# Cross-attention scores from full tiles: split keys and queries packed into 96 rows by way of HBM

## What is computed

```python
q = heads(rms_norm(hidden) @ cq_w, 16, 16)        # 16 heads of 16 dims, 112 queries
k, v = split(encoder_outputs @ ckv_w)             # 375 keys and values a batch
scores = einsum('bhqd,bhkd->bhqk', q / sqrt(16), k)
p = softmax(scores, axis=-1)
cross = einsum('bhqk,bhkd->bhqd', p, v) @ cdense_w
```

## Time and profile before

| | |
|---|---|
| median of 3 runs | 2347.46 us (2345.52 to 2348.16) |
| the profiled execution's own time | 2341.35 us |
| its span, first to last instruction | 2339.5 us |
| mean granted PE clock over the span | 0.982 |
| stage E, first group of scores of batch 0 to that of batch 31 | 539.7 us |

### The profile page before, as it was taken

The page is one execution under the profiler, slowest core; times in us unless marked ns, Lnnn a source line. Parts: engine busy times, 40 slices in busy tenths (PEclk is TensorE's granted clock), DMA queues, the critical chain, the costliest instruction groups (busy, mean ns, idle before and its releaser), DMA issues.

```text
span 2339.5 us, 46940 instructions
## 1 busy us (share of the span) xinstructions
PE 2202.4 (94%) x19542; PEld 1835.6 (78%) x19542; DVE 1338.8 (57%) x1919; ACT 1071.1 (46%) x1842; POOL 881.5 (38%) x738
## 2 busy tenths in 40 slices
PE   7999999999799999988999999997999999999998
PEld 6899987778666668877777777775888888888887
DVE  6656537787589975546666666663534444434332
ACT  5343434333177755534555555553543344334332
POOL 2210127767434324521222111110745455555553
PEclk9999999999899999988999999998999999999999
DMA  6343415556454446641111111102534344344331
GB/s 227 129 161 112 173 52 209 201 199 222 157 175 139 138 131 247 235 159 35 42 40 50 42 40 50 42 22 106 179 124 160 113 133 136 128 133 122 104 113 45
DMA packets 107602, 293.88 MB, mean 126 GB/s; under 512 B 14560, under 2 KB 19008, under 8 KB 100736
## 3 DMA queue, kind: packets, MB, share of 16 engines
q1 hardware_dynamic: 88672, 230.60, 29.9%
q0 software_dynamic: 18720, 60.29, 7.0%
HBM read 221.65 MB, written 69.18 MB: 124 GB/s over the span
## 4 chain that ended last, share of the span: by engine, by line
PE 79%; DVE 8%; ACT 7%; DMA 2%; issue 2%; POOL 1%; SPq 0%; POOLq 0%; DVEq 0%; ACTq 0%
PE ps L109 19%; PE ps L111 18%; PE ps L110 18%; PE ps L1625 4%; PE ps L1662 4%; PE ps L1644 3%; DVE f_arena L995 3%; ACT f_arena L1547 2%; PE ps L1164 2%; PE ps L627 2%; ACT f_arena L1112 1%; DVE f_arena L991 1%; PE ps L1175 1%; DVE f_arena L987 1%; ACT f_arena L1118 1%
## 5 line engine op out<-in xcount | busy, mean ns | idle before, releaser
L109 PE MATMUL ps<-r_arena 128*128 128x512 f32 (+6 forms) x2410 | 902.7, 375 | 28.4 <-DVE r_arena L177 14.2
L177 POOL TENSOR_TENSOR r_arena<-f_arena,r_arena 128x512 fp32r<-128x512 f32 (+1 forms) x438 | 589.1, 1369 | 857.9 <-ACT r_arena L1268 433.6
L111 PE MATMUL ps<-r_arena 128*128 128x512 f32 (+6 forms) x2410 | 882.6, 366 | 0.0
L110 PE MATMUL ps<-r_arena 128*128 128x512 f32 (+6 forms) x2410 | 882.1, 366 | 0.0
L109 PEld LDWEIGHTS ps<-r_arena 128*128 128x128 f32 (+2 forms) x2410 | 454.1, 188 | 120.8 <-issue 26.3
L111 PEld LDWEIGHTS ps<-r_arena 128*128 128x128 f32 (+2 forms) x2410 | 454.5, 189 | 66.2
L110 PEld LDWEIGHTS ps<-r_arena 128*128 128x128 f32 (+2 forms) x2410 | 455.0, 189 | 60.0
L199 ACT CAST r_arena<-f_arena 128x512 fp32r<-128x512 f32 x400 | 235.6, 620 | 172.6 <-PE ps L111 135.4
L1761 DVE TENSOR_REDUCE e_negmax<-ps 112x3 f32<-112x1125 f32 (+1 forms) x160 | 225.2, 1408 | 104.2 <-PE ps L1625 101.5
L1547 ACT ACTIVATE f_arena<-ps 125x1792 f32<-125x1792 f32 x96 | 159.8, 1665 | 98.3 <-PE ps L1647 97.8
L2047 DVE SCALAR_TENSOR_TENSOR f_arena<-f_arena,ps 128x512 f32<-128x512 f32 (+1 forms) x88 | 57.4, 652 | 235.2 <-ACT f_arena L1937 235.2
(11 more groups left out here) (201 smaller groups left out, 2738.3 us busy)
## 6 DMA issues: line engine op xcount, KB each, us to landing
f_arena<-weights SPq DMA_DIRECT2D x400, 256.0 KB, 3.0
f_arena<-rows SPq DMA_DIRECT2D x14, 1160.0 KB, 5.3
f_arena<-qk_rows SPq DMA_DIRECT2D x32, 448.0 KB, 3.9
f_arena<-mem_n SPq DMA_DIRECT2D x8, 1536.0 KB, 7.6
f_arena<-mem_e SPq DMA_DIRECT2D x32, 376.0 KB, 3.2
f_arena<-mem_t SPq DMA_DIRECT2D x16, 750.0 KB, 5.5
h_rows<-f_arena SPq DMA_DIRECT2D x7, 1160.0 KB, 4.8
f_arena<-h_rows SPq DMA_DIRECT2D x7, 1160.0 KB, 5.2
```

Source lines behind the costliest of these rows:

```text
L109: first = pe.matmul(out, w_hi, x_hi, start=start, stop=False)
L110: pe.matmul(out, w_hi, x_lo, start=False, stop=False)
L111: return first, pe.matmul(out, w_lo, x_hi, start=False, stop=stop)
L177: return engine.tensor_tensor(out, source, high.bitcast(F32), ALU.subtract)
```

## The change

Keys and queries of a batch are split once, into one pair of tiles (`e_kq_parts`, both scaled by 16 to the power of -1/4) without masks. SP writes the parts to two arrays in HBM (`k_rows`, `q_rows`) and reads them back in another arrangement: `e_keys` has, for each of the 8 head pairs, rows high, low, high of the even head (48 rows) and of the odd head (48 rows), `e_queries` rows high, high, low, with zeros for the other head's 48 rows. One matmul over 96 rows then adds all three products of a head. The columns of the key and query weights are permuted on the host so that a tile holds one parity of heads. The negative maxima go by a DMA into rows 96 and 97 of `e_queries` (the same rows of `e_keys` are ones), and a by-key matmul over 98 rows gives a pair of heads with its maxima.

```diff
-S_UNITS, KEY_UNITS = 5, 3
+S_UNITS, KEY_UNITS = 6, 6
+PAIRS, ROWS = HEADS // 2, 3 * CHD
+E_SCALE = float(CHD) ** -0.25
...
+        e_kq_parts = both(8192, (CT, CEVEN + SEQ))
+        e_keys = [rv(10144 + 3008 * i, (PAIRS, CEVEN)) for i in range(3)]
+        e_queries = [rv(at, (CT, PAIRS, SEQ)) for at in (4096, 5888, 19168)]
+        e_c_parts = both(20960, (CT, SEQ))
+        e_max_tok = [rv(25536 + 128 * i, (P,), SEQ) for i in range(2)]
+        e_max_t = rv(25792, (SEQ,))
+        key_units = [(t, c) for t in range(CT) for c in range(NKC)]
+        s_heads = [range(3 * u, 3 * u + 3) if u < 4 else range(2 * u + 4, 2 * u + 6) for u in range(S_UNITS)]
+        MAX_ROW = CT * ROWS
+        MAX_PLACES = 16
+
```

Four DMAs store a batch, eight place it, one places its maxima. Three buffers of each tile rotate:

```diff
+            def store(b, x, wide, into):
+                sp.dma_start(into[b, :, x].rearrange("t d (g s) -> (d g) t s", g=PAIRS), e_kq_parts[x][:, :, wide].bitcast(F32)).then_inc(
+                    e_stored.sem, 16)
+
+            def store_both(b):
+                for x, made in enumerate((e_kq_hi, e_kq_lo)):
+                    sp.wait_ge(made, e_split(b))
+                    store(b, x, keys, k_rows)
+                    store(b, x, queries, q_rows)
+
+            def place_keys(b):
+                sp.wait_ge(*stored(b))
+                into, done = e_keys[b % 3].rearrange("p g s -> p (g s)").bitcast(F32), e_placed[b % 2].sem
+                for t in range(CT):
+                    at = ROWS * t
+                    sp.dma_start(into[at:at + 2 * CHD], k_rows[b, t].rearrange("x d s -> (x d) s")).then_inc(done, 16)
+                    sp.dma_start(into[at + 2 * CHD:at + ROWS], k_rows[b, t, 0]).then_inc(done, 16)
+
+            def place_both(b):
+                if b < 3:
+                    sp.wait_ge(*e_cleared.at(1 if b == 1 else 3))
+                else:
+                    sp.wait_ge(e_st, KEY_UNITS * (b - 2))
+                place_keys(b)
+                into, done = e_queries[b % 3].rearrange("p t g s -> p t (g s)").bitcast(F32), e_placed[b % 2].sem
+                for t in range(CT):
+                    at = ROWS * t
+                    sp.dma_start(into[at:at + CHD, t], q_rows[b, t, 0]).then_inc(done, 16)
+                    sp.dma_start(into[at + CHD:at + ROWS, t], q_rows[b, t].rearrange("x d s -> (x d) s")).then_inc(done, 16)
+
+            def place_maximum(b):
+                sp.wait_ge(e_mxt_made, b + 1)
+                sp.dma_start(e_queries[b % 3][MAX_ROW:MAX_ROW + 2].bitcast(F32), e_max_t[0:2 * HEADS].bitcast(F32)).then_inc(
+                    e_max_placed.sem, 16)
+
...
             sp.wait_ge(*d_scattered.at(16 * BLOCKS))
             load_queries(0)
             load_queries(1)
+            place_keys(0)
+            sp.wait_ge(e_ones, 4 + 2 + 1)
+            sp.wait_ge(e_kq_hi, 2)
+            for row in (0, CHD):
+                place_queries(sp, row, e_kq_parts[0])
+            load_queries(2)
             base = sp.value_load(base_f[0:1, 0:1], min_val=W_F, max_val=W_F + F_CHUNKS)
-            for c in range(RING):
-                ring_load(sp, M_F + c, chunk_at(base, c))
-            for b in range(2, BATCHES):
-                load_memory(b)
-                load_queries(b)
+            store_both(1)
+            for s in range(BATCHES + 1):
+                if s + 4 < BATCHES:
+                    load_memory(s + 4)
+                if s + 3 < BATCHES:
+                    load_queries(s + 3)
```

```diff
                                         None).then_inc(e_scattered[b % 2].sem, 16)
 
+            e_memory_low(pool, 2)
+            pool.memset(e_queries[1].bitcast(F32), 0.0).then_inc(e_cleared.sem, 1)
+            pool.wait_ge(*e_cleared.at(1))
...
             for s in range(BATCHES + 2):
...
-                for x in range(2):
-                    dve.scalar_tensor_tensor(lo[:, :, x, :], ps[:, at:at + CT, CEVEN:CEVEN + SEQ], cmask[:, x:x + 1],
-                                             hi[:, :, x, :].bitcast(F32), ALU.mult, ALU.subtract).then_inc(e_kq_lo, 1)
+                dve.wait_ge(e_kq_hi, e_split(b) if wide.stop > CEVEN else 1)
+                dve.scalar_tensor_tensor(e_kq_parts[1][:, :, wide], ps[:, at:at + CT, wide], E_SCALE,
+                                         e_kq_parts[0][:, :, wide].bitcast(F32), ALU.mult, ALU.subtract).then_inc(e_kq_lo, 1)
```

The two kinds of scores, in 6 groups of heads (3, 3, 3, 3, 2, 2) and 6 by-key units of 4 matmuls. A unit uses two PSUM banks, in turn, so it waits for the unit two before it:

```diff
                 if u == 0:
-                    pe.wait_ge(e_kq_lo, 3 * (b + 1))
+                    pe.wait_ge(*placed(b))
                     if b == 0:
+                        pe.wait_ge(e_kq_lo, 2)
                         pe.wait_ge(e_v_act, 1)
                         pe.wait_ge(e_v_dve, 1)
                 if S_UNITS * b + u:
                     pe.wait_ge(e_maxed, S_UNITS * b + u)
-                if u == S_UNITS - 1 and b >= 2:
...
+                for h in s_heads[u]:
+                    last = pe.matmul(ps[0:SEQ, h - s_heads[u][0], 0:CEVEN], e_queries[b % 3][0:MAX_ROW, h % 2, h // 2, :],
+                                     e_keys[b % 3][0:MAX_ROW, h // 2, :], start=True, stop=True)
                 last.then_inc(e_s, 1)
...
             def scores_by_key(b, u):
...
+                    if b < 3:
+                        pe.wait_ge(*e_cleared.at((2, 4, 5)[b]))
+                    pe.wait_ge(*e_max_placed.at(MAX_PLACES * (b + 1)))
+                    pe.wait_ge(e_kq_lo, e_split(min(b + 3, BATCHES - 1)))
+                if u == 1:
+                    pe.wait_ge(e_v_act, min(b + 4, BATCHES))
+                    pe.wait_ge(e_v_dve, min(b + 4, BATCHES))
+                if b or u >= 2:
+                    pe.wait_ge(e_exp, KEY_UNITS * b + max(u - 1, 0))
+                t, c = key_units[u]
+                m = slice(c * KC, (c + 1) * KC)
+                for n in range(PAIRS // 2):
+                    pair = PAIRS // 2 * t + n
+                    last = pe.matmul(ps[0:KC, 4 + 2 * (u % 2) + n // 2, n % 2 * 2 * SEQ:(n % 2 + 1) * 2 * SEQ],
+                                     e_keys[b % 3][0:MAX_ROW + 2, pair, m], e_queries[b % 3][0:MAX_ROW + 2, :, pair, :],
+                                     start=True, stop=True)
                 last.then_inc(e_st, 1)
```

The maxima are written once into a tile of 128 columns instead of four times, and `maximum_turned` is a copy of 112 columns. ACT takes the exponentials of a batch in six instructions of 896 columns, the output's copy standing between the fourth and the fifth. PE's loop, which now splits keys two batches ahead and does both halves of a context together:

```diff
+            for s in range(BATCHES + 2):
+                old, now, new, by_key = s >= 2, s < BATCHES, s + 2 < BATCHES, 1 <= s <= BATCHES
+                if now:
+                    scores(s, 0)
+                if old:
+                    context(s - 2, 0)
+                    context(s - 2, 1)
...
+                if by_key:
                     maximum_turn(s - 1)
-                scores(s, 1)
-                if s >= 2:
-                    context(s - 2, 1)
-                if 2 <= s + 1 < BATCHES:
-                    values(s + 1, range(1))
-                if s >= 2:
+                if now:
+                    scores(s, 1)
+                if old:
...
+                if new:
+                    e_key_products(pe, s + 2)
+                if old:
                     back(s - 2)
-                scores(s, 2)
-                if s:
+                if now:
+                    scores(s, 2)
+                if new:
+                    queries_turn(s + 2)
+                    values(s + 2, range(NKC))
+                if now:
+                    scores(s, 3)
+                if by_key:
                     scores_by_key(s - 1, 0)
-                if s >= 2:
+                    scores_by_key(s - 1, 1)
+                if old:
                     dense(s - 2, 0)
-                scores(s, 3)
-                if s >= 2:
+                if by_key:
+                    scores_by_key(s - 1, 2)
+                if now:
```

```diff
+                if now:
+                    scores(s, 4)
+                if by_key:
+                    scores_by_key(s - 1, 3)
+                if old:
                     dense(s - 2, 1)
...
+                if now:
+                    scores(s, 5)
+                if by_key:
+                    scores_by_key(s - 1, 4)
+                    scores_by_key(s - 1, 5)
```

More of the change, by code:

```diff
@@ L1485, in build_xattn, with e_split, placed, stored @@
         e_out = [fv(18016 + 512 * i, (DIM,), SEQ) for i in range(2)]
-        e_k_parts = [both(8192 + 1504 * i, (CT, CEVEN)) for i in range(3)]
-        e_q_parts = [both(12704 + 896 * i, (QUADS, SEQ)) for i in range(3)]
-        e_c_parts = both(15392, (CT, SEQ))
-        e_max_tok = [rv(16288 + 128 * i, (4, 2 * HEADS), SEQ) for i in range(2)]
-        e_max_t = rv(16544, (QUADS, SEQ))
-        key_units = [[(0, 0), (0, 1)], [(0, 2), (1, 2)], [(1, 0), (1, 1)]]
-        s_heads = [range(3 * u, 3 * u + 3 if u < S_UNITS - 1 else HEADS) for u in range(S_UNITS)]
+        e_kq_parts = both(8192, (CT, CEVEN + SEQ))
[8 more added lines that the diff above has]
+        MAX_PLACES = 16
+        def e_split(b):
+            return b + 2
+        def placed(b):
+            return e_placed[b % 2].at(16 * (8 * (b // 2 + 1) + (2 if b % 2 == 0 else 0)))
+        def stored(b):
+            return e_stored.at(16 * (2 + 4 * b))
+        keys, queries = slice(0, CEVEN), slice(CEVEN, CEVEN + SEQ)
```

(26 more changed lines are left out.)

251 lines of the change are left out of this document (110 added, 141 removed).

## The result

The changed kernel takes 2288.98 us in the median of 4 runs (2287.28 to 2293.10), the kernel before 2347.81 in the median of 4 runs taken with it; the ratio is 0.9753, with a 95% interval of 0.9736 to 0.977. The forecast was 2283, faster; the range holds the result. So the two traces differ by 48.2 us of span, the medians by 58.8.

The account below looks back on a forecast made before the run. PE was taken to set the pace. 29 batches at 15.5 instead of 17.5 us give -58, start and end -6.4, together -64; from the median of 2347.46 the forecast is 2283 us, range 2258 to 2325.

Parts of the forecast that it names:

- The pass, 15.5 us: Steady batch on PE: 17.50 us falls to 15.5, with bounds 15.0 and 16.1.
- The short waits: New PE waits at reduces, between passes and before contexts: 0.25 us a batch in all.
- The rest of the pass: Keys, values, contexts, transposes and dense on PE: same instructions in another order, 10.01 us a batch.
- The rounds: Score matmuls on PE: 0.24 us per round of three 32-row tiles against 0.17 per full matmul, a gain of 0.6.
- The DMA: Added stores and placements in stage E: share 0.72, placement landing at 12 of 15.5 us, hidden with 3 to spare.
- Rival 2: Placement before a batch's scores is late, bound by partition: up to 20.3 us a batch, 2422 us; 18 in 100.
- Start and first passes: Stage E's beginning: first scores 2.7 us later, first two passes 26.5 us in place of 32.2, so -5.7.
- one more DMA (2.08 again): Start of stage E: batch 0's queries go through one further DMA of 2.08 us before the first scores.
- chains of reduces: First two passes, without contexts: reduces of 11.4 us and some 2 of other DVE work, 26.5 for both.
- The end, -3.4,: From the last batch's first scores to the last dense matmul: 35.5 us in place of 38.9.
- Rival 1: PE waits at several of the six reduces and at the contexts: 16.5 us a batch, 2312 us; 17 in 100.
- rival 3: By-key units still wait for each exponential in full: no change, within 5 us of 2347; 3 in 100.

Follow-up runs that it names:

- the first experiment: Changed kernel with by-key units again in pairs over all four banks, each next pair waiting for both exponentials; full tiles stay: 2349.69 us, 1.0008 of the kernel before.
- the second store: Changed kernel with each batch's split keys stored a second time, to another HBM array that nobody reads: 2325.01 us.
- another start: Changed kernel with batch 0's queries all placed from ACT's DMA queue and batch 1 split into tiles of its own: 2288.72 us.
- the new order and fillers: Changed kernel with score group five before by-key unit 2, six before dense's second half, and unused matmuls in passes 0, 1, 30 and 31: 2275.56 us, ratio 0.9718.

## Why the prediction was right

**The pass, 15.5 us.** Measured 15.36 in the steady passes, 15.53 in the mean of passes 2 to 30. A head's full matmul costs 0.17 as foreseen; a by-key matmul 0.109, between the bounds of 0.105 and 0.12. Two terms were off, and they nearly cancel. The short waits are 1.0 us a pass (0.3 at the exponential, 0.3 and 0.4 at reduces), where the forecast took 0.25. The rest of the pass is 9.0 us (15.36 - 2.72 - 2.62 - 1.04), where it took 10.01, since both halves of a context stand together (2.44 us from 1290.39 to 1292.83, where the halves took some 2.7) and the weight port idles at two changes of tiling a pass and not at six. That the sum came within 0.2 us is in part luck. That the gain hangs on the wait, the first experiment shows.

**The rounds, a reading that was wrong.** The prediction divided 0.71 us by three rounds, got 0.24 against 0.17 for a full matmul, and concluded that the tiles themselves gain 0.6 us by the rows. The 0.71 contains the 0.25 of idle weight port that the prediction itself names. Without it a round starts 0.17 us after the last. So 15 rounds before (three for each of the five groups) and 16 matmuls now stream 2.55 and 2.72 us: the full tiles lose 0.2 there, and gain at the changes of tiling.

**The DMA, the step that failed in size.** The forecast took 293 GB/s for the full share and got 0.72; measured are 0.89 to 0.90 at 218 GB/s. From the totals, 174 GB/s were added for 0.74 of the share, so the new transfers run at 235 GB/s. That rate leaves out any effect of the old and the new transfers on each other. The placement was to arrive 12 us into a pass of 15.5, with 3 to spare; it arrives 14.6 to 15.1 us into it in most passes, and 15.4 in the one of the chain (1274.25 to 1289.65). The cover of 3 us did not exist; 0.1 to 0.7 us to the last reduce are left. Rival 2's price for the placement alone, 15.1 us into the pass, came within 0.6 us of all of them; its sequel, that the other transfers push it to 16.1 and the time above that of before, did not come. Whether the partitions or the engines are the limit is open: with the second store the placement comes later because it is issued later, so that run doesn't decide it. A run that places the same bytes into more partitions was not made.

**Start and first passes.** +6.8 instead of +2.7, and +2.8 instead of -5.7. The step "one more DMA (2.08 again)" failed: a placement of short runs between tiles takes 6.6 us, not the 2.08 of a load of 112 KB. In "chains of reduces" two things were left out. Pass 0 is 17.1 us: batch 1 goes through the whole detour bare: it is split when batch 0's placement has landed (1052.59), stored, placed, and lands at 1069.64. With this off the path (another start) pass 0 still took 16.0, so the detour is not all of it. Pass 1 is 17.2 us, with matmuls at the lower of the clock's two levels (keys 0.31 apart, granted 0.70); with the new order and fillers it takes 13.2 at 1.00, which is what the forecast had for it. These 12 us are what lies between the forecast gain of 64 and the 52.5 of the trace. The medians differ by 58.8, nearer to the forecast than the stage is; the 6 us more are no part of this account, and no trace shows where they lie. So that the median came as near to 2283 as it did is partly luck.

**The end, -3.4,** measured -4.3. POOL's five `ring_low` run from 1574.15 to 1580.3 and its next task starts at 1582.50: hidden, with 2 us to spare, as said.

**Rival 1** (handoffs, 16.5 us a pass) came in small, 0.3 and 0.4 us at two of the six reduces, and did not reach its price; rival 3 is excluded by the trace. The rule that row tiles work in parallel (the Trainium skill, TensorEngine Tiling (Array Packing), Tiling Modes) was set aside by the prediction for the rows. The trace bears it out, with rounds of three tiles 0.17 us apart. The loss of 0.7 us a pass that the prediction worked out from it supposed rounds of four, and four of the five groups had three heads.

## What to carry to other kernels

Before a matmul is made denser, look at what PE waits for between the matmuls, and measure a round from start to start, not up to the next kind of matmul: that distance contains the change of tiling. Here a unit that takes half the banks, so that the exponential of one runs beside the matmuls of the next, carries a good half of the gain of a pass. A detour through HBM is free as long as its whole chain (stores, placements, the small one they queue behind) lands within one pass; follow it to its landing, since a share of 0.89 left 0.1 to 0.7 us here and the share alone does not tell this. Take the rates of runs of the same length, not those of long ones. A wait is put down to the engine that reported last, so check it against a run without that engine's work. When work is taken out of a pass, or moved, ask what it covered.

## What the runs showed that was not expected

- Passes with less work were longer: 17.1 and 16.4 us against 15.36, with PE's granted clock at 0.79 and idle stretches of about 1.5 us in them; useless matmuls in these gaps made them 15.0 and 13.8.
- 96 matmuls of both context halves in a row take 2.44 us, and each change from full matmuls to these costs the weight port 0.25 us. The six idle places of this kind in a batch of the kernel before cost 1.6 us, as much as its wait for the exponential (1.5).
- 0.77 MB more a pass, 23% of the bytes, raised the DMA share only from 0.89 to 0.96, but cost 1.5 us a pass, and the pass got longer with them.
